# The last feed-forward of a two-layer vision block: masked inputs and stacked experts in place of slots in device memory

## What is computed

```python
logits = x @ gate_w + gate_b                      # x: layer-normalised tokens, 1024 x 64
idx = argmax(softmax(logits)); prb = softmax(logits)[idx]
one_hot = one_hot(idx, 8)
pos = (cumsum(one_hot, axis=0) * one_hot).sum(-1) - 1
kept = pos < C_cap                                # C_cap = ceil(1.25 * 1024 / 8) = 160
buf[idx, pos] = x                                 # 8 experts x 160 slots, dropped beyond
hmid = relu(buf @ w1 + b1)                        # 64 -> 256
ybuf = hmid @ w2 + b2                             # 256 -> 64
y = ybuf[idx, min(pos, C_cap - 1)] * (prb * kept)
out = residual + nan_to_num(y, 0, 1e4, -1e4)
```

## Time and profile before

| | us |
|---|---|
| median of 3 runs | 301.6 (300.65 to 302.51) |
| the profiled execution | 301.3 |
| its span in the trace | 299.6 |
| last feed-forward, from the logits' copy (L1503) to the end | 54.8 |

### The profile page before, as it was taken

The page is one execution under the profiler, slowest core; times in us unless marked ns, Lnnn a source line. Parts: engine busy times, 40 slices in busy tenths (PEclk is TensorE's granted clock), DMA queues, the critical chain, the costliest instruction groups (busy, mean ns, idle before and its releaser), DMA issues.

```text
span 299.6 us, 2884 instructions
## 1 busy us (share of the span) xinstructions
PE 211.1 (70%) x888; PEld 130.0 (43%) x888; DVE 189.2 (63%) x476; ACT 57.8 (19%) x97; POOL 141.4 (47%) x187
## 2 busy tenths in 40 slices
PE   0959298979977979888927686988998840079300
PEld 0735296743444722245313333666778430039200
DVE  7768879978947394554069399998862457003116
ACT  1413733210010283341020000101012030012100
POOL 5400047959905139311028479999980113700171
PEclk9999789999985599999996599999999985559855
DMA  3538990000000000000390000000000000010111
GB/s 119 176 67 171 206 194 2 0 0 4 0 1 0 0 1 3 0 0 0 91 206 2 1 0 0 0 4 0 0 0 2 0 1 9 26 44 2 44 26 44
DMA packets 8317, 10.86 MB, mean 36 GB/s; under 512 B 4651, under 2 KB 5163, under 8 KB 8235
## 3 DMA queue, kind: packets, MB, share of 16 engines
q1 hardware_dynamic: 7788, 10.14, 14.7%
q0 software_dynamic: 512, 0.53, 0.7%
HBM read 8.05 MB, written 2.61 MB: 36 GB/s over the span
## 4 chain that ended last, share of the span: by engine, by line
DVE 31%; PE 29%; POOL 17%; issue 15%; ACT 5%; DMA 2%; DVEq 1%; POOLq 0%; ACTq 0%
POOL ring L269 11%; PE ps L924 5%; PE ps L782 3%; PE ps L764 3%; PE ps L894 3%; DVE ps L1160 3%; DVE big L283 2%; POOL slots_in L556 2%; PE ps L717 2%; PE ps L950 2%; DVE ring L291 2%; DVE cm L1107 2%; DVE xn L1063 2%; POOL rstd L443 2%; PE ps L831 2%
## 5 line engine op out<-in xcount | busy, mean ns | idle before, releaser
L269 POOL TENSOR_TENSOR ring<-big 128x384 f32<-128x384 f32 x72 | 59.1, 856 | 8.8 <-PE ps L924 3.9
L301 POOL TENSOR_TENSOR big<-big 128x512 f32<-128x512 f32 x30 | 32.0, 1096 | 35.6 <-ACT big L628 29.8
L924 PE MATMUL ps<-ring,ident 128*128 128x384 f32 x100 | 38.0, 525 | 9.6 <-POOL ring L269 5.6
L709 PE MATMUL ps<-zero,ident 128*128 128x512 f32 x34 | 22.9, 825 | 16.9 <-DMA slots_in<-xn,idx_in 15.2
L764 PE MATMUL ps<-ring,ident 128*128 128x192 f32 x126 | 25.9, 357 | 8.6 <-DVE ring L291 8.4
L1466 DVE TENSOR_TENSOR ps<-ps,ring 128x384 f32<-128x384 f32 x46 | 25.8, 562 | 9.6 <-PE ps L924 8.4
L924 PEld LDWEIGHTS ps<-ring,ident 128*128 128x128 f32 x100 | 19.1, 202 | 25.6 <-DVE ring L269 6.7
L764 PEld LDWEIGHTS ps<-ring,ident 128*128 128x128 f32 x126 | 22.1, 205 | 12.8 <-DVE ring L291 12.8
L443 POOL TENSOR_TENSOR rstd<-veps,mhalf 128x4 f32<-128x4 f32 x8 | 8.3, 1041 | 40.0 <-DVE veps L1059 39.9
L269 DVE TENSOR_TENSOR ring<-big,ps 128x384 f32<-128x384 f32 x36 | 19.5, 546 | 0.1
L709 PEld LDWEIGHTS ps<-zero,ident 128*128 128x128 f32 x34 | 8.2, 260 | 25.2 <-DMA slots_in<-xn,idx_in 15.3
(11 more groups left out here) (270 smaller groups left out, 375.8 us busy)
## 6 DMA issues: line engine op xcount, KB each, us to landing
big<-pad SPq DMA_DIRECT2D x8, 392.0 KB, 9.3
big<-pad SPq DMA_DIRECT2D x8, 240.0 KB, 5.4
w<-in_w_dram SPq DMA_DIRECT2D x1, 520.0 KB
w<-in_w_dram SPq DMA_DIRECT2D x2, 256.0 KB
pad<-img SPq DMA_DIRECT2D x8, 64.0 KB, 2.1
w<-in_w_dram SPq DMA_DIRECT2D x1, 512.0 KB
pad<-zero SPq DMA_DIRECT2D x1, 484.0 KB, 3.8
pad<-zero SPq DMA_DIRECT2D x1, 400.0 KB, 4.3
```

The costliest lines, as they stand in the source:

```text
L269: return eng.tensor_tensor(V(ring, 0, slot * SP, [[1, P], [NJ * C, 3], [C1, NJ * G1], [1, C1]]), bigv((py + dy) * SLAB1 + (dx + j0) * C, [ ...
L301: return eng.tensor_tensor(dst, bigv(wy * SLAB0 + wx * C, [C0, J * G0], [1, C0]), table, ALU.mult)
L709: mm(bank(free_bank, 0, P, [1, 512]), ident[:, :], zero[:, 0:512], start=True, stop=True)
L924: mm(bank(1 + i % 2, 0, P, [1, SP]), ident[:, :], ring[:, slot * SP:slot * SP + SP], start=(n == 0), stop=(n == len(srcs) - 1)).then_inc(s ...
```

## The change

The slots are gone. The input of each expert is instead the whole token matrix with the tokens of other experts set to zero:

- `xn` is written twice side by side, so that a transposed block has the 64 channels on partitions 0 to 63 and again on 64 to 127. The one-hot of each token's expert is written in bf16 (`oh_parts`), and TensorE spreads it over partitions: the upper half of a mask belongs to expert 2i, the lower half to expert 2i + 1. The first two masks come from 16 small matmuls; the other six from one bf16 matmul of 512 columns each, after the one-hot was transposed and copied out by ScalarE. VectorE multiplies inputs by masks (`mask_inputs`, eight times).
- Two experts are stacked on the 128 partitions. `chosen_hidden` accumulates the four pairs in the same PSUM banks, two matmuls of 512 columns for each of four pairs and two halves of the tokens. Only the chosen expert contributes. The biases come from the one-hot times `b1_parts` (three bf16 parts).
- After a ReLU on ScalarE, the second product takes one block of 128 tokens as the stationary side and all eight experts' w2 side by side (512 columns) as the moving side; VectorE multiplies that by the token's weight for each expert, which is zero for all but one (`weigh`). The eight blocks of 64 are summed by GpSimd for six token blocks and by VectorE for the last two.
- The finish with its NaN handling and the store run in four pieces of two blocks.
- GpSimd prepares the bias parts ahead of `inv_std(5)`: six casts and three subtractions of 8 x 320 elements. `keep_clock(2, 7)` now stands behind the gate's product. The clearing of `slots_in` and of `w_11` is gone; two small bf16 tiles are cleared instead. SyncE loads the same weights in another layout, and three copies of the biases.

Its core:

```diff
-            sp.dma_start(V2(slots_in, [[ST_N * C, P], [1, ST_N * C]]), zero[:, 0:ST_N * C]
-                         ).then_inc(sem("slots_zeroed"), 16)
...
+            sp.dma_start(b_g1[:, :], V2(a["w_g1"], [[0, P], [1, E]], off=C * E)).then_inc(sem("w_ffn1"), 16)
+            load(w_11[:, :, :], "w_11", "w_ffn1")
...
-            for weights in (w_i1[:, :, :], w_11[:, :], cw_parts[:, :, :]):
+            for weights in (w_i1[:, :, :], cw_parts[:, :, :], oh_parts[:, :, :], b1_parts[:, :]):
...
+            pool.wait_ge(sem("w_ffn1"), W_FFN1)
+            pool.wait_ge(sem("w_u"), 3)
+            for part in range(NPART):
+                r = slice(32 * part, 32 * part + E)
+                for _ in range(part):
+                    step(gp.tensor_copy(b1_parts[r, :], b_1[r, :]))
+                    step(gp.tensor_tensor(b_1[r, :], b_1[r, :], b1_parts[r, :], ALU.subtract))
...
             inv_std(5)
...
-            for j in range(J):
-                gp.indirect_dma_start(out=slots_in.ap(), out_offset=bass.IndirectOffsetOnAxis(
-                    ap=idx_in[:, j:j + 1], axis=0), in_=xn[:, j, 0, :], in_offset=None
-                ).then_inc(sem("scattered"), 16)
...
+            for j in range(POOL_JOINS):
+                pool.wait_ge(sem("y_prod"), j + 1)
+                base = YP + 512 * (j % YP_SLOTS)
+                for half in (4 * C, 2 * C):
+                    step(gp.tensor_tensor(bigv(base, [1, half]), bigv(base, [1, half]), bigv(base + half, [1, half]), ALU.add))
+                gp.tensor_tensor(ysum[:, j, :], bigv(base, [1, C]), bigv(base + C, [1, C]), ALU.add
+                                 ).then_inc(sem("joined"), 1)
...
+            act.wait_ge(sem("ohT_ps"), 1)
+            sc.copy(cwT[0:BROWS, :, :], cwT_bank(5, p=BROWS)).then_inc(sem("ohT"), 1)
             gate_exp(2)
...
+            last.then_inc(sem("gate_ps"), 2)
+            keep_clock(2, 7)
...
+            def expert_masks(u):
+
+                hf, i = divmod(u, E // 2)
+                if u >= 2:
+                    pe.wait_ge(sem("x_masked"), u - 1)
+                if u < 2:
+                    for j in range(HJ):
+                        for n in range(2):
+                            last = mm(bank(6 + u, C * n, C * n + C, [1, P], off=j * P),
+                                      V(oh_parts, 0, j * BROWS + 2 * i + n, [[1, P], [0, C]]), ident_bf[:, :],
+                                      start=True, stop=True)
+                else:
+                    pe.wait_ge(sem("ohT"), 1)
+                    last = mm(bank(6 + u % 2, 0, P, [1, 512]), pick_half[:, i * P:i * P + P],
+                              cwT[0:E, HJ * hf:HJ * hf + HJ, :], start=True, stop=True)
+                last.then_inc(sem("mask_ps"), 1)
+
+            def chosen_hidden(u):
+
+                hf, i = divmod(u, E // 2)
+                pe.wait_ge(sem("x_masked"), u + 1)
+                for f in range(2):
+                    mm(bank(2 * hf + f, 0, P, [1, 512]), w_11[:, i, P * f:P * f + P], bigv(XM + 512 * u, [1, 512]),
+                       start=(i == 0), stop=False, skip_group_check=True)
...
+            for u in range(E):
+                if u + 2 < E:
+                    expert_masks(u + 2)
+                chosen_hidden(u)
...
+            for j in range(J):
+                pe.wait_ge(sem("h1"), 2 * (j // HJ) + 2)
+                if j >= len(Y_BANKS):
+                    pe.wait_ge(sem("y_prod"), j - len(Y_BANKS) + 1)
+                for f in range(2):
+                    last = mm(bank(Y_BANKS[j % len(Y_BANKS)], 0, P, [1, E * C]), bigv(H1 + f * J * P + j * P, [1, P]),
+                              w_21[:, f, :], start=(f == 0), stop=(f == 1))
+                last.then_inc(sem("y_ps"), 1)
...
-            layernorm(4, x3, 1e-5, 1, residual3)
+            layernorm(4, x3, 1e-5, 2, residual3)
...
+            def mask_inputs(u):
+
+                dve.wait_ge(sem("mask_ps"), u + 1)
+                v.tensor_tensor(bigv(XM + 512 * u, [1, 512]), bigv(XN2 + 512 * (u // HJ), [1, 512]),
+                                bank(6 + u % 2, 0, P, [1, 512]), ALU.mult).then_inc(sem("x_masked"), 1)
...
+            def weigh(j):
+
+                dve.wait_ge(sem("y_ps"), j + 1)
+                if j >= YP_SLOTS:
+                    dve.wait_ge(sem("joined"), min(j - YP_SLOTS + 1, POOL_JOINS))
+                v.tensor_tensor(bigv(YP + 512 * (j % YP_SLOTS), [C, E], [1, C]),
+                                bank(Y_BANKS[j % len(Y_BANKS)], 0, P, [C, E], [1, C]),
+                                V(cw, 0, j * E, [[1, P], [1, E], [0, C]]), ALU.mult).then_inc(sem("y_prod"), 1)
+
+            def finish(cols):
+
                 j0, nj = cols.start, cols.stop - cols.start
+                if j0 < POOL_JOINS:
+                    dve.wait_ge(sem("joined"), cols.stop)
...
+            for j in range(J):
+                weigh(j)
+                if j >= POOL_JOINS:
+                    dve.wait_ge(sem("y_prod"), j + 1)
+                    step(v.tensor_reduce(ysum[:, j, :], bigv(YP + 512 * (j % YP_SLOTS), [1, C], [C, E]), AX.X, ALU.add))
+                for cols, at in zip(LAST, FINISH_AT):
+                    if at == j:
+                        finish(cols)
...
-LAST = (slice(0, 5), slice(5, J))
+LAST = (slice(0, 2), slice(2, 4), slice(4, 6), slice(6, J))
+FINISH_AT = (3, 5, 6, 7)
+POOL_JOINS = 6
+Y_BANKS = (6, 7, 0, 1)
```

More of the change, by code:

```diff
@@ L996, in _ @@
             keep_clock(3, 4)
-            transposes(5, normalised, "xn", 3)
-            pe.wait_ge(sem("w_ffn1"), 64)
-            project(w_g1[:, :], 4, E, "gate_ps", 5, slot=E)
-            pe.wait_ge(sem("tri"), 1)
-            pe.wait_ge(sem("tot"), 1)
-            mm(bank(5, 0, P, [1, E]), tri[:, :], total1[:, :], start=True, stop=True).then_inc(sem("before"), 1)
-            pe.wait_ge(sem("scattered"), 16 * J)
-            keep_clock(2, 6)
-            pe.wait_ge(sem("slots_loaded"), 16)
@@ new lines, in _ @@
+            chosen_bias(1)
+            for j in range(J):
+                pe.wait_ge(sem("h1"), 2 * (j // HJ) + 2)
[5 more added lines that the diff above has]
+                last.then_inc(sem("y_ps"), 1)
@@ L1286, in first_of_max @@
                 step(v.tensor_reduce(den[:, :], je(t1), AX.X, ALU.max))
+                if early is not None:
+                    v.tensor_tensor(early, je(t1), bc(den), ALU.is_equal).then_inc(sem("oh_bf"), 1)
                 step(v.tensor_tensor(je(dst), je(t1), bc(den), ALU.is_equal))
```

226 lines of the change are left out of this document (89 added, 137 removed).

## The result

| | before | changed |
|---|---|---|
| median of 9 runs each, us | 301.6 (300.65 to 303.6) | 300.49 (298.54 to 300.85) |
| profiled execution, its span, us | 301.3, 299.6 | 299.95, 298.2 |
| from the logits' copy to the end, us | 54.8 | 48.8 |

The ratio is 0.9943, with a 95% interval of 0.9917 to 0.997. The forecast was 296.3; its sign held, its size did not, and the median lies just outside the range. Counted from the logits' copy, the last stage is 6.0 us shorter, where 6.7 was forecast (54.8 to 48.1). It begins 4.6 us later, where 1.4 was forecast.

The account below looks back on a forecast made before the run. The last feed-forward was taken as bound by a chain of DMAs; in its place, steps reaching 246.2, 253.5, 269.8, 276.9, 292.2 and 294.3, plus 1.7 around the span and 0.3 to the median, gave 296.3 us, range 291.5 to 300.0.

Parts of the forecast that it names:

- end of the gate: Last gate: small matmuls, the last eight slowed by the clock's fall, end at about 246.2 us on the span's clock.
- from there to the first wide matmul: Behind the gate: one-hot, clock holders, masks, transposes and ScalarE's copy; first wide matmul at 253.5 us.
- first product: Last stage on TensorE: wide passes 13.8, five more masks 1.0, bias matmuls 0.8, small ones and count 0.7; sum 16.3 us.
- to the fourth weighing: Second product on TensorE: four passes, 1.72 us a block; the fourth block is there at 276.9 us.
- VectorE's tail: From the fourth block on, VectorE's weighings, sums and four finishes have more to do than 1.72 us a block: 15.3 us.
- GpSimd's bias parts: In front of inv_std(5): nine operations take 5.5 us, making the deviation and the whole second layer 0.7 us late.
- middle case: Last gate: clock falls before the holders and is back before the wide matmuls; 296.3 us, chance 0.52.
- the late case: Rival, first product: clock comes back late, eight passes at half clock, +3.4 us, giving 299.7; chance 0.12.
- The case without a fall: Rival, last gate to masks: the clock never falls, 3.3 us less, giving 293.0; chance 0.2.
- the chain through device memory: Last feed-forward: scatter, gathers and slot DMAs between the one-hot and VectorE's first five blocks, 44.6 us, go.
- the holders stand in the one-hot's way: Ahead of the masks: four holder passes at half clock end at 249.8, 2 us after the one-hot is there.
- the 3 of the rival: Rival, tail: VectorE and GpSimd block each other fully, three more us for the first finish, giving 300; chance 0.1.

Follow-up runs that it names:

- experiment 1: Changed kernel with GpSimd's bias preparation moved from ahead of inv_std(5) to behind inv_std(6); 298.81 us, ratio 0.9855 to the kernel before.
- experiment 8: Changed kernel with keep_clock(1, 7) in place of keep_clock(2, 7) behind the last gate; 298.88 us, ratio 0.9867 to the kernel before.
- experiment 14: Kernel before plus only GpSimd's bias block, on unused zeros, in front of inv_std(5); 302.7 us, ratio 1.0032 to the kernel before.
- experiment 9: The changed kernel run once more, unchanged, beside the kernel before; 299.84 us, ratio 0.993.
- experiment 12: Changed kernel with keep_clock(5, 4) in place of keep_clock(3, 4) ahead of the last transposes; 295.82 us, ratio 0.9783 to the kernel before.
- experiment 16: Changed kernel with bias parts later, two finishes, keep_clock(5, 4) ahead of the last transposes, keep_clock(6, 4) at the start; 294.22 us, ratio 0.9729; again 294.39, 0.9746.
- experiment 7: Changed kernel with the finish in two pieces of four blocks in place of four of two; 297.69 us, ratio 0.9838 to the kernel before.
- experiment 5: Changed kernel with the start of the kernel before restored (a DMA ahead of w_out's load, more clearing); 299.09 us, ratio 0.9896 to the kernel before.
- experiment 13: Kernel before with keep_clock(5, 4) in place of keep_clock(3, 4) ahead of the last transposes; 301.74 us, ratio 1.0007.
- experiment 10: The kernel before run once more, unchanged, for one profile; 303.67 us.

## Why the prediction was wrong

**The sum by its own steps.** Forecast and the changed kernel's profile, us:

| step | forecast | measured |
|---|---|---|
| end of the gate | 246.2 | 249.31 |
| from there to the first wide matmul | 7.3 | 6.3 |
| first product | 16.3 | 17.6 |
| to the fourth weighing | 7.1 | 7.1 |
| VectorE's tail | 15.3 | 15.9 |
| store and end | 2.1 | 2.0 |

The last stage was forecast at 48.1 from the gate's end and took 48.9. That it came so near is in part luck: the way to the first wide matmul was 1.0 shorter than forecast, since the masks and transposes ran at full clock again, and the first product 1.3 longer. Of 3.9 us that the span is off, 3.1 had come before it.

**The step that failed** is the one on GpSimd's bias parts: "so the deviation is 0.7 late, and the whole second layer with it". GpSimd's part of it was right. The block took 5.6 (forecast 5.5), the norm came 0.87 later (forecast 0.7), and experiments 1, 8 and 14 give 0.87, 0.84 and 0.80. What failed is the assumption under the sum: that all other work upstream of the change would take as long as in the one profile of before. The lateness of the logits' copy was put at 1.4 us and measured 4.6. The clock of TensorE falls at places that differ between executions of the same program. Upstream of the logits this moved the kernel before itself by 2.4 us (244.79 and 247.16), and it moved the changed kernel and its one-holder variant, equal up to there, by 3.5 at the second convolution's copy (235.78 and 232.31). The profile of before had an execution without the fall at the first offset product, the profile after one with that fall and with another at 143.6. In the single runs of the kernel before on one chip the time goes with the mean granted clock: four runs at 0.871 took 300.0 to 301.0, three at 0.852 took 303.9 to 304.9.

One unlucky profile is not the whole account, though, for the median of nine runs missed too (298.54 to 300.85, none at the forecast). Six profiles of the changed kernel and its variants with four finishes and no holders added ahead of the last gate, and without the delay, have their logits anywhere from 246.88 to 249.58, and yet their spans are 297.8 to 299.0 in every one: what experiment 8 won upstream it lost behind the gate. The forecast joined the upstream of one execution to the gate of another, and no profile shows both.

**The last gate's clock was treated the same way.** "That stretch is there in the changed kernel too" was right, but what I listed as rivals differs from one execution to the next. The forecast's middle case is the profile after and experiment 9 (stage 48.8 and 49.4); the late case stood only in experiment 8 (51.0), which has one holder less. The case without a fall did not occur in any profile with `keep_clock(3, 4)`; with the two more holders it did in two of four (experiments 12 and 16), and in the other two the clock was back 3.4 us after its fall. The rival's sum for it gave a span of 291.0, experiment 12 has 293.0. At equal upstream, experiments 8 and 12 lie 4.9 us apart (297.9 and 293.0), and both differ from the changed kernel only in holders; these are single profiles, and the two extremes. Against the middle case the clock at this gate is worth 1.5 to 3.3 us (experiment 12), as much as the changed kernel's whole gain of 1.1 to 1.7 us or more. But the forecast had counted the middle case, so this is no part of its miss.

**Right:** the chain through device memory goes (54.8 to 48.8), TensorE doesn't wait for VectorE's masked inputs, VectorE's backlog ends the program (experiment 7), the holders stand in the one-hot's way, and the joins stay under a block's 1.72. **Smaller errors:** the one-hot came 2.0 us behind the logits' copy, not 1.5. A third and later mask is busy for 0.38 on TensorE, not 0.2, and costs more than that:

```profile
260.20 1.98 PE L1014 MATMUL ps<-big,w 128*128 128x512 f32 x4
262.11 0.38 PE L1005 MATMUL ps<-cwT,pick_half 8*128 8x512 bf16 x1
262.43 1.98 PE L1014 MATMUL ps<-big,w 128*128 128x512 f32 x4
...
267.56 5.42 PE L1014 MATMUL ps<-big,w 128*128 128x512 f32 x12
272.81 0.60 PE L1020 MATMUL ps<-cwT,b_parts 72*128 72x512 bf16 x2
```

From start to start a pair with its mask takes 2.23 (260.20 to 262.43), while twelve passes in an unbroken row take 5.25, or 1.75 for four. So a mask costs 0.48, and five of them are 1.4 us more than forecast, which is all of the first product's 1.3. The finish beside the joins took 2.9 and 3.3 (forecast 3.0 and 2.6) and 2.15 alone. In the rows of the last stage L1577 takes 0.66 where a join began 0.15 ahead of it, and 0.23 alone: it ends within 0.1 us of that join's first instruction (0.73). Over a finish the joins cost 0.8 to 1.15 us, not the 3 of the rival. The Trainium skill ("SBUF — State Buffer", section "Who interferes with whom") says that a `tensor_scalar` in a two-port mode and a GpSimd instruction exclude each other for the whole instruction of whoever came first. The row of L1577 agrees, if it ran in such a mode, which no row states.

**Open:** the fall at the first offset product, worth 1.5 to 1.7 us, stood in 9 of 11 profiles of the changed kernel's family with four or five holders there, and in 1 of 6 of the kernel before's. Experiment 8 shows that it is not fixed by the program. But if it were equally likely in both, so uneven a split would come up in about 2 of 100 cases (an estimate from these counts), so it is probably likelier in the changed kernel, and then it is a cost of the change that I did not find the cause of. Experiment 5 speaks against the start's work, with one profile. The interval of experiment 12 rests on three runs.

## What to carry to other kernels

Before a sum is built on one profile, mark where the clock fell in it: such a place can differ from one execution to the next, and a second profile of the same kernel tells how far upstream times move (here 2.4 us, more than the change's whole effect). When a change puts dense TensorE work right behind a stretch of small matmuls, the clock there can go from costing nothing that shows (experiment 13) to costing 1.5 to 3.3 us (experiment 12), and holders in TensorE's idle time ahead of the stretch are part of the change. A slower stage may also be one's own holders: place them where TensorE waits anyway, not between a result and the work that needs it.

## What the hardware showed

- The clock falls some time after light work, under whatever runs then: in the changed kernel at 249.4, as the holders began, 5.6 us of idle time and small matmuls after the last holders had ended at 243.8. At the start, with eight or ten passes of holders and then 1.9 to 3.6 us idle, it fell in 10 of 17 profiles; with twelve passes and 0.8 to 0.9 us idle in neither of two. The idle time alone does not decide: the clock fell after 1.9 us of it (experiment 10) and stayed up after 3.1 (experiment 8).
- A bf16 matmul of 512 columns between fp32 ones was busy for 0.38 and put off what followed by 0.48; two in a row were busy for 0.60.
- Nine dependent GpSimd operations on 8 partitions x 320 elements: a cast 0.44, a subtraction 0.79. That a subtraction goes by the elements of a partition, and not by the 8 partitions, fits: 384 elements on 128 partitions took 0.86.
